# One of eight products per scan chunk moved from VectorE to GpSimd, in a decoder layer on one core

## The reference, cut to what matters

```
delta = softplus((x @ W_dtw.T) @ W_dt.T + b_dt)      # 128 channels
Bm = x @ W_B.T ;  Cm = x @ W_C.T                     # 16 states each
A = -exp(A_log)
def step(h, inp):
    d_t, b_t, c_t, x_t = inp
    dA = exp(d_t[..., None] * A)
    h = dA * h + d_t[..., None] * b_t[:, None, :] * x_t[..., None]
    y_t = sum(h * c_t[:, None, :], axis=-1)
```

## Time and profile before

| | |
|---|---|
| median of three runs | 678.48 us (676.48 to 686.47) |
| the profiled execution, own time | 678.42 us |
| its span, first to last instruction | 676.8 us |
| scan stage, first product to last scan | 24.2 to 255.1 us |
| mean granted TensorE clock | 0.872 |

### The profile page before, as it was taken

The page is one execution under the profiler, slowest core; times in us unless marked ns, Lnnn a source line. Parts: engine busy times, 40 slices in busy tenths (PEclk is TensorE's granted clock), DMA queues, the critical chain, the costliest instruction groups (busy, mean ns, idle before and its releaser), DMA issues.

```text
span 676.8 us, 10788 instructions
## 1 busy us (share of the span) xinstructions
PE 534.8 (79%) x3387; PEld 379.0 (56%) x3387; DVE 426.4 (63%) x862; ACT 321.8 (48%) x727; POOL 370.6 (55%) x301
## 2 busy tenths in 40 slices
PE   2579999898998988887564699797979699999800
PEld 0234445344453545776454588686867588989800
DVE  1599999999999991368668765556635422222254
ACT  2474676867768643332122155454625133333327
POOL 1487979899897964213455633626363533322360
PEclk9999999999999989555555599798989799999955
DMA  5334434454544525544234947343636465789574
GB/s 154 129 123 159 152 130 154 149 186 138 169 165 137 201 97 98 110 71 75 55 78 79 237 154 211 99 163 107 197 101 194 142 200 183 234 276 302 192 261 115
DMA packets 77175, 104.51 MB, mean 154 GB/s; under 512 B 40784, under 2 KB 56400, under 8 KB 76992
## 3 DMA queue, kind: packets, MB, share of 16 engines
q1 hardware_dynamic: 71504, 90.99, 45.1%
q0 software_dynamic: 4320, 8.92, 3.9%
q10 hardware_dynamic: 1296, 3.93, 1.6%
HBM read 91.48 MB, written 12.34 MB: 153 GB/s over the span
## 4 chain that ended last, share of the span: by engine, by line
PE 32%; POOL 21%; issue 16%; DVE 12%; DMA 6%; ACT 3%; another core or an unknown queue 2%; SPq 1%; DVEq 0%; POOLq 0%; ACTq 0%
POOL hc L646 13%; PE pB L1071 10%; PE pq L1084 5%; PE py L826 4%; PE pa L987 3%; PE py L1071 3%; POOL y_dram L753 2%; DMA dx<-in_ctx_T 2%; PE pq L1054 1%; POOL xg_dram L744 1%; DMA Crep<-c_dram 1%; POOL bc_rest L602 1%; POOL bcs L610 1%; DMA y_dram<-dx,xin 1%
## 5 line engine op out<-in xcount | busy, mean ns | idle before, releaser
L646 POOL TENSOR_TENSOR hc<-h,Crep 128x1024 f32<-128x1024 f32 x64 | 149.6, 2354 | 16.2 <-DVE h L1515 14.8
L753 POOL DMA_INDIRECT y_dram<-dx,xin x71 | 68.7, 967 | 136.6 <-ACT dx L1386 127.8
L826 PE MATMUL py<-hc,ident 128*128 128x512 f32 x256 | 122.2, 605 | 7.9 <-POOL hc L646 7.9
L1071 PE MATMUL pB<-Crep,wslot 128*128 128x256 f32 (+1 forms) x556 | 114.5, 350 | 11.9 <-issue 9.6
L1071 PEld LDWEIGHTS pB<-Crep,wslot 128*128 128x128 f32 x556 | 88.0, 200 | 27.9 <-issue 13.3
L1506 DVE TENSOR_TENSOR u<-dx,pC 128x1024 f32<-128x1024 f32 x64 | 77.2, 1206 | 18.4 <-PE pC L815 18.3
L826 PEld LDWEIGHTS py<-hc,ident 128*128 128x128 f32 x256 | 47.4, 191 | 54.9 <-issue 38.8
L1515 DVE TENSOR_TENSOR_SCAN h<-pB,u 128x1024 f32<-128x1024 f32 x32 | 73.1, 2283 | 1.0 <-ACT pB L1204 0.6
L1515 DVE TENSOR_TENSOR_SCAN h<-pa,u 128x1024 f32<-128x1024 f32 x32 | 73.0, 2282 | 0.0
L1797 DVE TENSOR_TENSOR u<-u,pB 128x512 f32<-128x512 f32 x36 | 24.8, 688 | 72.8 <-PE pB L1071 40.1
L1797 DVE TENSOR_TENSOR Crep<-u,pB 128x512 f32<-128x512 f32 x35 | 24.1, 687 | 67.4 <-PE pB L1071 45.5
(11 more groups left out here) (225 smaller groups left out, 950.9 us busy)
## 6 DMA issues: line engine op xcount, KB each, us to landing
wslot<-in_expert_w SPq DMA_DIRECT2D x46, 768.0 KB
Crep<-c_dram SPq DMA_DIRECT2D x64, 512.0 KB, 3.8
h<-m_dram SPq DMA_DIRECT2D x16, 256.0 KB
xin<-xg_dram SPq DMA_DIRECT2D x25, 130.0 KB, 4.1
cT_st<-in_ctx_T SPq DMA_DIRECT2D x8, 256.0 KB, 4.2
dx<-in_ctx_T SPq DMA_DIRECT2D x8, 256.0 KB
delta<-in_ctx_tok SPq DMA_DIRECT2D x32, 64.0 KB
hc<-y_dram SPq DMA_DIRECT2D x8, 256.0 KB, 6.6
```

Source lines behind the costliest of these rows:

```text
L646: nc.gpsimd.tensor_tensor(hc[:, K % 4], h[:, K % 3], Crep[:, K % 4].rearrange("p a t -> p (a t)"), ALU.mult).then_inc(hc_done, 1)
L753: nc.gpsimd.indirect_dma_start(out=y2_dram, out_offset=bass.IndirectOffsetOnAxis(ap=xin[:, i % NX, a, D:D + 1].bitcast(i32), axis=0), in_= ...
L826: last = nc.tensor.matmul(py[:], ident[:], hc[:, K % 4, i * CH:(i + 1) * CH], start=False, stop=(K % STEPS == STEPS - 1 and i == 1))
L1071: last = nc.tensor.matmul(bank[:, o * a * P:(o + 1) * a * P], wslot[:, i % NW, stage * F + f * P:stage * F + (f + 1) * P], xgT[i % 2][:, 0 ...
```

## The change

In each chunk the product of step k = 4 (`U4`) is done by POOL in place of DVE. POOL cannot read the PSUM tile, so the two rows of B reach it by a broadcast load like those of C: `store_C` now stores all 32 rows of `bc_raw`, and `load_B` fills `Brep`, a part of an expert-weight buffer that is free in this stage. PE leaves out `spread_B` of that step. On POOL the order becomes w0, w1, product_4, split_rest, w2, split_lo, and from there as before. `spreads(K)` counts the products of DVE before step K.

```
-        c_dram = nc.dram_tensor("c_dram", (NCH, N, CH), f32, kind="Internal").ap()
+        c_dram = nc.dram_tensor("c_dram", (NCH, N2, CH), f32, kind="Internal").ap()
+        def spreads(K):
+            return K - (K + STEPS - 1 - U4) // STEPS
 (SP)
-                sp.dma_start(c_dram[c], bc_raw[N:N2]).then_inc(C_stored, 16)
+                sp.dma_start(c_dram[c], bc_raw[:]).then_inc(C_stored, 16)
+            def load_B(c):
+                sp.wait_ge(C_stored, 16 * (c + 1))
+                if c:
+                    sp.wait_ge(u4_done, c)
+                sp.dma_start(Brep, c_dram[c:c + 1, 2 * U4:2 * U4 + 2].broadcast_to([P, 2, CH])).then_inc(B_in, 16)
             store_C(0)
+            load_B(0)
...
                     if k == 4 and c + 1 < NCH:
                         store_C(c + 1)
+                    if k == 5 and c + 1 < NCH:
+                        load_B(c + 1)
 (POOL)
+            def product_4(c):
+                K = STEPS * c + U4
+                pool.wait_ge(B_in, 16 * (c + 1))
+                pool.wait_ge(dx_done, c + 1)
+                if K >= 3:
+                    pool.wait_ge(h_done, K - 2)
+                nc.gpsimd.tensor_tensor(u[:, K % 3].rearrange("p (a t) -> p a t", a=2),
+                                        dx[:, c % 2].unsqueeze(1).to_broadcast([P, 2, CH]), Brep, ALU.mult).then_inc(u4_done, 1)
...
                     weigh_state(STEPS * c + k)
+                    if k == U4 - 3:
+                        product_4(c)
...
-                        if k == 0:
+                        if k == 1:
                             split_rest(c + 1)
 (PE)
-                    if K + 2 < STEPS * NCH:
+                    if K + 2 < STEPS * NCH and (K + 2) % STEPS != U4:
                         spread_B(K + 2)
 (DVE)
+                if K % STEPS == U4:
+                    dve.wait_ge(u4_done, K // STEPS + 1)
+                else:
+                    dve.wait_ge(u_done, spreads(K) + 1)
...
-                    if K + 1 < STEPS * NCH:
+                    if K + 1 < STEPS * NCH and (K + 1) % STEPS != U4:
                         product(K + 1)
```

More of the change, by code:

```diff
@@ L196, in decoder_layer @@
         xgT = (Crep[:, 2, 1, 0:PAIR], Crep[:, 2, 1, PAIR:])
+        Brep = wslot[:, 0, 0:2 * CH].rearrange("p (a t) -> p a t", a=2)
         sil = u[:, 1].rearrange("p (a f) -> p a f", a=2)
@@ L257, in decoder_layer @@
         B_spread = sem("B_spread")
+        B_in = sem("B_in")
+        u4_done = sem("u4_done")
         a_ready = sem("a_ready")
@@ L372, in decoder_layer @@
         BARE = 5
+        U4 = 4
+        def spreads(K):
+            return K - (K + STEPS - 1 - U4) // STEPS
         def close_wait(engine):
@@ L457, in load_C @@
                     sp.wait_ge(hc_done, K - 3)
-                sp.dma_start(Crep[:, K % 4], c_dram[c:c + 1, 2 * k:2 * k + 2].broadcast_to([P, 2, CH])).then_inc(C_in[K % 4], 16)
+                sp.dma_start(Crep[:, K % 4], c_dram[c:c + 1, N + 2 * k:N + 2 * k + 2].broadcast_to([P, 2, CH])).then_inc(C_in[K % 4], 16)
+            def load_B(c):
[3 more added lines that the diff above has]
+                sp.dma_start(Brep, c_dram[c:c + 1, 2 * U4:2 * U4 + 2].broadcast_to([P, 2, CH])).then_inc(B_in, 16)
             def load_context(c):
@@ L495, in load_heads @@
                 else:
-                    sp.wait_ge(u_done, STEPS * NCH)
+                    sp.wait_ge(u_done, spreads(STEPS * NCH))
                 sp.dma_start(cTc, ctx_T[:, tokens(c)]).then_inc(heads_loaded, 16)
@@ L626, in make_dx @@
                 if c >= 2:
-                    pool.wait_ge(u_done, STEPS * (c - 1))
+                    pool.wait_ge(u_done, spreads(STEPS * (c - 1)))
+                    pool.wait_ge(u4_done, c - 1)
                 nc.gpsimd.tensor_tensor(dx[:, c % 2], delta[:, c % 2], xT[:, tokens(c)], ALU.mult).then_inc(dx_done, 1)
@@ L640, in weigh_state @@
                     pool.wait_ge(BC_lo_done, K // STEPS + 1)
-                if K % STEPS == 1 and K // STEPS + 1 < NCH:
+                if K % STEPS == 2 and K // STEPS + 1 < NCH:
                     pool.wait_ge(BC_rest_done, K // STEPS + 2)
@@ L812, in spread_B @@
                 if K:
-                    pe.wait_ge(u_done, K)
+                    pe.wait_ge(u_done, spreads(K))
                 for i in range(2):
@@ L1185, in keep_BC @@
                 if c >= 2:
-                    act.wait_ge(B_spread, STEPS * (c - 1))
+                    act.wait_ge(B_spread, spreads(STEPS * (c - 1)))
                 nc.scalar.copy(bcs[0:N2, c % 2], bc_raw[:]).then_inc(BC_hi_done, 1)
@@ L1501, in product @@
                 c = K // STEPS
-                dve.wait_ge(B_spread, K + 1)
+                dve.wait_ge(B_spread, spreads(K) + 1)
                 dve.wait_ge(dx_done, c + 1)
@@ L1511, in scan @@
                 dve.wait_ge(a_ready, K + 1)
-                dve.wait_ge(u_done, K + 1)
+                if K % STEPS == U4:
+                    dve.wait_ge(u4_done, K // STEPS + 1)
+                else:
+                    dve.wait_ge(u_done, spreads(K) + 1)
                 if K >= 3:
```

## The result

The changed kernel takes 677.62 us (median of 20 runs, 675.02 to 686.32). In the same comparison the kernel before takes 681.96 us (20 runs, 676.48 to 686.47), so the median of the three runs shown ahead of the prediction, 678.48, was a low one. The ratio is 0.9958, with a 95% interval of 0.9938 to 0.9977. That is 2.9 us gained, 1.6 to 4.2 us. The two medians alone differ by 4.3 us, a little outside this interval; this text goes by the ratio. The forecast, 675.1 against 678.42 us, is a ratio of 0.9951.

The account below looks back on a forecast made before the run. The bound was taken to be a loop through POOL, PE and ACT, 28.04 us a chunk after the change against 28.36. 678.42 - 1.6 (to w4 of chunk 6) - 1.75 (last chunk) = 675.1 us; 8-in-10 range 670 to 681.

Parts of the forecast that it names:

- DVE has about 1.8 us to spare: Scan stage: a chunk needs 26.5 us of DVE against 28.36 us, so DVE isn't the bound.
- (c): DVE loses one product in eight and PE one spread; the 1.11 us are worth nothing in chunks 0 to 6.
- (a): split_rest leaves its place before w1, so POOL's wait for ACT there, 2.8 us a chunk, goes.
- (b): product_4 adds one POOL instruction between w1 and w4, taken at 2.32 us, bounds 2.3 and 4.6.
- I give it nothing, with 0.2 us a chunk as its bound: ACT's split_mid, behind the later split_rest: the decay for k = 5 is still there about when its scan wants it.
- The sum over chunks 0 to 6, 1.6 us: w4 of chunk 6 starts at 219.1 instead of 220.72, some 1.6 us gained.
- The last chunk, 1.75 us: The skip term no longer waits for DVE's product of k = 4: 1.75 us sooner, bounds 0 and 2.9.
- load_B costs nothing: One more 512 KB load beside eight, landing in 3.8 us, at most 6.7, delays nothing.
- The gain is eaten: Rival: PE's queue or ACT's later split gives the gain back, DVE holds the last chunk's; 678 to 679 us, chance 0.2.
- DVE was the bound after all: Rival: each chunk saves its 1.11 us of DVE, 8.9 us in all, so 669.5 us; chance 0.12.
- POOL dearer: Rival: product_4 on POOL's loop makes the kernel slower; 681 us in a lesser form (0.13), 691 if held off (0.05).

Follow-up runs that it names:

- order_back: Changed kernel with split_rest back in its old place before w1, product_4 still on POOL; ratio 1.0207 to the kernel before, period 30.55 us.
- order_only: Changed kernel's order, split_rest behind w1, but all eight products on DVE; ratio 1.0052 to the kernel before.
- tiny_old: Changed kernel with POOL's product on 8 of 512 tokens and split_rest back in its old place; ratio 0.9974 to the kernel before.
- tiny_new: Changed kernel, new order, with POOL's product on only 8 of 512 tokens; ratio 0.9958 to the kernel before, period 27.88 us.
- early_new: Changed kernel with all of POOL's constants written before the first chunk; ratio 0.9927 to the kernel before.
- last_only: Kernel before, in its old order, with product_4 and load_B in the last chunk alone; ratio 0.9971 to the kernel before.
- early_old: Kernel before with all of POOL's constants written before the first chunk; ratio 1.0005 to the kernel before.

## Why the prediction was right or wrong

The direction and the size of the whole were near: 675.1 us forecast as 3.35 us under the kernel before, 2.9 us measured. The absolute time is 2.5 us above the forecast, since the level it was set against was a low draw. Two steps of the reasoning failed. One is the reading of what bounds the kernel, where DVE's load was put at nothing. The other is ACT's later split, put at nothing too, which cost 0.9 us in chunk 2. By parts:

| part | forecast | measured |
|---|---|---|
| from w4 of chunk 0 to w4 of chunk 1 | 0.9 | 0.8 |
| from w4 of chunk 1 to w4 of chunk 6 | 0.7 | 0.13 |
| last chunk | 1.75 | 1.6 |

- **"DVE has about 1.8 us to spare", and (c) "DVE is not the bound, so the 1.11 us are worth nothing in chunks 0 to 6"**: this step failed. The prediction has one loop, through POOL, PE and ACT. order_back shows that this loop is there (30.55 us). But a second one, through DVE's eight products and scans, ACT's scale_rows_p and PE's gate_products, is as long. DVE's idle time was not to spare: it lies in the wait for PE, on the loop. With the order alone the chunk stays at 28.36 us (order_only), with the lighter DVE alone at 28.44 (tiny_old), with both it is 27.88 or 27.92. So in the new order the saved product is worth 0.48 us a chunk and not nothing. The chunk's length came out all the same, since what was summed up was POOL's loop, and with DVE's shortened it is POOL's that is left: 28.04 us forecast, 27.92 measured. In this the sum came out by luck: it left DVE's loop out, and the change happened to shorten that one too.
- **(a) the wait for split_rest goes**: right, 16.9 us to 0.0.
- **(b) product_4 at 2.32 us**: right, 2.348 us without a wait. What it costs is another thing. Against the same kernel without it (tiny_new) it costs 0.04 us a chunk, because it fills a wait for ACT's split_mid that the new order would otherwise have. I named that queue, and said that what is late next is w1's own input. tiny_new shows that split_lo's input is as late.
- **(b) "I give it nothing, with 0.2 us a chunk as its bound"**: the other step that failed. In chunks 4 to 6 it holds. Into chunk 2, split_lo waits 1.13 us for ACT and the period is 29.93 us, where 29.0 was forecast (105.2 - 76.2). The lists of PE and ACT in the changed kernel show where it comes from:

```profile
89.32 1.05 PE L899 MATMUL pq<-center,xT 128*128 128x128 f32 x8
...
92.46 1.04 PE L836 MATMUL pq<-xT,wbc 128*32 128x512 f32 x2
```

```profile
93.54 0.57 ACT L1213 COPY bc_raw<-pq 32x512 f32<-32x512 f32 x1 [2.54 <-PE pq L836]
...
98.76 0.60 ACT L1223 CAST bc_mid<-bc_rest 32x512 bf16<-32x512 f32 x1
```

  The scan of k = 1 starts at 88.09 us there, and BC_product (line 836) 4.37 us after it. PE's products that centre rows stand ahead of it. In chunk 5, which has none, it is about 2.6 us. ACT's copy waits for BC_product, split_mid comes 5.2 us behind the copy, and split_lo after that. I had worked out ACT's queue for a late chunk and used it for all, although in the kernel before the distance is 4.38 us in chunk 2 as well. This costs 0.9 us once. It is there in early_new (29.93 us) and order_only (29.94) as well. That the centring products are the cause is read from the lists; no run moves them.
- **The sum over chunks 0 to 6, 1.6 us**: measured 0.8 us by the two profiles (220.72 to 219.92). The place of the mark in chunk 0 differs by over 1 us between profiles of one kernel (48.13 and 49.17 for the changed one), so distances tell more. From w4 of chunk 0 to w4 of chunk 1 it is 29.02 us in both profiles of the kernel before and 28.21 and 28.19 in those of the changed one, 0.8 us gained. The order does this: order_only has 28.19 there and tiny_old 29.21. From w4 of chunk 1 to w4 of chunk 6 the gain is 0.13 us: 0.34 and 0.43 in the last two periods and 0.12 in the first, less 0.14 into chunk 3 and 0.62 into chunk 4. Into chunk 4 POOL's constants are on the bound, as forecast: 29.4 us, measured 29.28. Into chunk 3 the number, 28.5 forecast and 28.40 measured, was luck, since the reason isn't POOL alone: without its constants that chunk is as long (28.38). The constants themselves had been read about 0.05 us too long each (1.39, 0.88 and 1.76 us by the earlier trace rows, not 1.45, 0.92 and 1.82). The parts that repeat come to 2.5 us, of the 2.9 that were measured.
- **The last chunk, 1.75 us**: right, 36.50 to 34.90 is 1.6 us. last_only gives the same 34.90 without the rest. This is more than half of what the change gains. The profile I started from had 38.19 us there, with 1.7 us of lower clock that I took for part of the kernel. It didn't enter the sum, but my upper bound of 2.9 us, "if the sums behind it also run faster than now", had room for it.
- **load_B costs nothing**: right. product_4 never waits, and its load lands in 3.8 us like the others.
- **Rivals.** "The gain is eaten" holds in the loop for chunks 1 to 4, and not in the last. "DVE was the bound after all", at 8.9 us, falls with tiny_old, which saves the product on DVE and is no shorter in the loop. But DVE's loop was a bound beside POOL's, and neither the rivals nor the sum had two at once. "POOL dearer" falls at 2.348 us. Its place, product_4 on the loop, is real once the order is undone (order_back). The rule of the Trainium skill, Perfetto Trace Analysis, Optimizing Scalar/DVE Operations, on the shared port doesn't show here: weigh_state lasts 2.356 us beside a DVE that is busy nearly all the time, against 2.355 in the earlier trace rows, and product_4 2.348. Both of DVE's instructions here have one input in PSUM, the case that the prediction sets apart.

What stays open is why order_only, whose undisturbed chunks are as long as before, is slower than the kernel before as a whole. Its two profiles have six separate stretches of lower clock in the scan stage, and those of the old order (five profiles: before twice, last_only, tiny_old, early_old) have one in all; order_back, whose order is old too, has one at 40 to 48 us. In the first look two of them make their chunks 1.7 us longer each (30.07 against 28.36), which is about the size of the 0.5%. Whether the order itself brings them on was not tested by a run made for it. But the traces point that way, as the end shows: in order_only PE waits ahead of gate_products in nine chunks of ten, and in the kernel before in none.

## What to carry to other kernels

Look for a second loop before you call an engine's idle time spare. Where two loops are equally long, each edit alone gains nothing, and idle time that ends in a wait on the loop is part of it. Moving work to an engine that is also on the loop can be free if that engine has a wait inside the loop. Find the wait, name what releases it, and price the moved instruction by how far it overfills the wait, not by its own length. Read the queue of each releasing engine for every kind of chunk, the early and the last ones too, since one term holds only where the same work stands ahead of it. Read a period on more than one engine: one that was late by chance catches up, and a short chunk behind a disturbed one isn't the length of the loop. And look at a second profile of the kernel before where a stage seems long, because a stretch of lower clock looks like structure in one.

## What the runs showed of the hardware

TensorE's clock falls to its lower level (1.2 of 2.4 GHz) for a few microseconds in the midst of a busy stage, at a different place from run to run. PE in order of time in the first profile of the changed kernel:

```profile
115.19 0.36 PE L919 MATMUL pq<-gk,x1T_all 128*128 128x8 f32 x2 [0.34 <-issue]
...
116.75 0.37 PE L920 MATMUL pq<-gkv,cT_st 128*128 128x8 f32 x2
116.97 0.69 PE L845 MATMUL pC<-bcs,sel 96*128 96x512 bf16 x2
117.45 3.53 PE L856 MATMUL py<-hc,ident 128*128 128x512 f32 x4
```

The same four matmuls of sum_state took 1.88 us at 112.98 us. The windows of that run give busy time of each engine and the granted clock (the last column but two):

```profile
112.00:116.00 4.00, 3.66 (x21) 2.22 (x19) 3.46 (x3) 2.36 (x6) 4.00 (x10) 1.00 0.55 208
116.00:120.00 4.00, 4.00 (x16) 2.27 (x16) 3.09 (x4) 2.42 (x10) 4.00 (x3) 0.67 0.64 211
```

Before it fell PE had waited 0.34 us and then done the sixteen 8-column matmuls of gate_products. Over all fourteen profiles, chunks 2 to 6, gate_products ran 70 times. Ahead of 28 of them PE had waited 0.34 to 1.0 us, and 10 of these 28 were followed by the lower clock in the very next group of sum_state. Ahead of the other 42 it had not waited, and none was followed by it. All 28 are in kernels with the new order. The remaining stretches of the scan stage follow a wait of PE too, for DVE's product (1.39 to 1.71 us) or for POOL (at 40 to 48 us). This is a count over traces; no run sets the wait and changes nothing else. In the last chunk of the kernel before, it had waited 1.71 us for DVE (PE in order of time, first profile, then the second profile):

```profile
239.04 0.59 PE L815 MATMUL pC<-bcs,sel 96*128 96x512 bf16 x2 [1.71 <-DVE u L1506]
...
240.71 5.02 PE L826 MATMUL py<-hc,ident 128*128 128x512 f32 x8
```

```profile
239.53 0.59 PE L815 MATMUL pC<-bcs,sel 96*128 96x512 bf16 x2 [1.73 <-DVE u L1506]
...
240.94 3.60 PE L826 MATMUL py<-hc,ident 128*128 128x512 f32 x8
```

The same wait stands ahead of both, and only one of them is followed by the lower clock, with 1.4 us lost in one group of matmuls. Such a stretch cost 1.7 us here in the last part (38.19 against 36.50), 1.2 us in the first profile of the changed kernel (29.57 against 28.40 into chunk 3), 1.7 in tiny_new (29.57 against 27.88) and 1.7 in order_only (30.07 against 28.36 into chunk 6), and nothing that shows by w4 of chunk 1 in the changed kernel's second profile, where it lay at 40 to 48 us. For a change worth 3 us, one profile of each kernel can't settle the sum. The distances between marks of undisturbed chunks that follow an undisturbed one repeat to some 0.03 us and can.

After the opening load the time to the end differs as well, for one and the same kernel: 418.0 and 424.0 us in the two profiles of the kernel before, 420.7 and 427.6 in the two of the changed one. Among the changed kernel's runs the time goes with the mean granted clock (675.0 us at 0.869, 686.3 at 0.862). This profile's other 2.9 us lie within that spread, which is why the ratio of many runs was needed.
